# Feed-forward over its inner channels in blocks of 128 in place of 256

## The reference, cut to what matters

```
residual = h
h2 = rmsnorm(h, ln2_w)                                      # (2048, 512)
mlp = jax.nn.silu(h2 @ gate_w) * (h2 @ up_w) @ down_w       # gate, up: (512, 2048); down: (2048, 512)
return residual + mlp
```

## Time and profile before

| | before |
|---|---|
| runs, median (lowest to highest) | 1661.74 us (1661.30 to 1663.65) |
| the profiled execution's own time | 1666.47 us |
| its span, first to last instruction | 1664.8 us |
| mean granted TensorE clock | 0.942 |
| PE busy | 1445.6 us, 87% |
| DVE, ACT, POOL busy | 780.0, 446.8, 441.1 us |
| feed-forward, first matmul to last statistics | 658.4 to 1198.7 us |

### The profile page before, as it was taken

One profiled execution on the slowest core, in us unless ns is written; L12 is line 12 of the kernel. 1 busy time (PEld: TensorE's weight loads), 2 busy tenths in 40 slices (PEclk: granted clock), 3 DMA queues, 4 the chain that ended last, 5 costly groups with the idle time before them and its releaser, 6 DMA issues. The chain is left out here.

```text
span 1664.8 us, 20088 instructions
## 1 busy us (share of the span) xinstructions
PE 1445.6 (87%) x6651; PEld 1045.3 (63%) x6652; DVE 780.0 (47%) x1357; ACT 446.8 (27%) x924; POOL 441.1 (26%) x486
## 2 busy tenths in 40 slices
PE   5688979769999994999999999999760599999996
PEld 4566768536666663888888888888620355555553
DVE  4857676658998992323232323233544122122121
ACT  4333434345555552212112121121120111111110
POOL 2411111126776764101011111010006222222222
PEclk9899999979999997999999999999985799999998
DMA  8112202352332314801000010000197222223220
GB/s 179 51 51 102 101 28 100 127 171 89 107 116 96 121 58 170 289 17 32 20 25 25 16 34 17 22 0 0 53 364 262 87 78 86 87 82 86 89 77 21
DMA packets 92867, 147.12 MB, mean 88 GB/s; under 512 B 29182, under 2 KB 45566, under 8 KB 92800
## 3 DMA queue, kind: packets, MB, share of 16 engines
q1 hardware_dynamic: 79424, 119.92, 22.0%
q0 software_dynamic: 8800, 25.21, 4.5%
q10 hardware_dynamic: 4576, 1.13, 0.3%
HBM read 91.63 MB, written 58.27 MB: 90 GB/s over the span
## 5 line engine op out<-in xcount | busy, mean ns | idle before, releaser
L1356 PE MATMUL ff_bank<-ff_hT_hi,ff_w_hi 128*128 128x512 f32 x512 | 202.3, 395 | 13.3 <-POOL ff_w_lo L1262 13.3
L1356 PE MATMUL ff_bank<-ff_hT_hi,ff_w_lo 128*128 128x512 f32 x512 | 204.9, 400 | 0.0
L1356 PE MATMUL ff_bank<-ff_hT_lo,ff_w_hi 128*128 128x512 f32 x512 | 203.0, 396 | 0.0
L1797 PE MATMUL ex_bank<-w_gu,xT 128*128 x624 | 193.5, 464 | 1.4 <-ACT xT L1728 0.8
L1322 DVE TENSOR_TENSOR ff_prod<-ff_prod,ff_bank 128x512 f32<-128x512 f32 x64 | 44.0, 688 | 274.7 <-PE ff_bank L1356 266.3
L1262 POOL TENSOR_TENSOR ff_w_lo<-ff_stage,ff_w_hi 128x1024 fp32r<-128x1024 f32 x24 | 57.3, 2393 | 417.2 <-ACT ff_w_hi L1309 413.6
L1797 PEld LDWEIGHTS ex_bank<-w_gu,xT 128*128 128x128 f32 x624 | 116.7, 192 | 60.9 <-issue 3.8
L1767 DVE SCALAR_TENSOR_TENSOR result_rows<-ex_bank,xs,result_rows 128x512 f32<-128x512 f32 x39 | 29.3, 751 | 256.2 <-DMA result_rows<-out_dram,xs 253.6
L479 DVE SCALAR_TENSOR_TENSOR conv_acc<-raw,conv_w,conv_acc 128x512 f32<-128x512 f32 x144 | 114.9, 799 | 62.4 <-ACT raw L296 52.5
L572 PE MATMUL pj_bank<-hT_hi,w_in_hi 128*128 128x512 f32 x336 | 140.3, 418 | 1.6 <-DVE hT_lo L412 1.6
L572 PE MATMUL pj_bank<-hT_lo,w_in_hi 128*128 128x512 f32 x336 | 137.5, 409 | 0.0
(11 more groups left out here) (238 smaller groups left out, 2429.9 us busy)
## 6 DMA issues: line engine op xcount, KB each, us to landing
cv_rows<-cst SPq DMA_DIRECT2D x12, 1024.0 KB, 4.3
cv<-cv_rows SPq DMA_DIRECT2D x16, 768.0 KB, 4.3
sorted_rows<-blank SPq DMA_DIRECT2D x1, 10023.0 KB, 46.0
xs<-sorted_rows SPq DMA_DIRECT2D x39, 257.0 KB, 2.7
zs_rows<-zst SPq DMA_DIRECT2D x8, 1024.0 KB, 6.5
zs<-zs_rows SPq DMA_DIRECT2D x16, 512.0 KB, 5.3
w_gu<-in_L_ffn_Wg_dram SPq DMA_DIRECT2D x8, 704.0 KB, 10.7
w_gu<-in_L_ffn_Wu_dram SPq DMA_DIRECT2D x8, 704.0 KB, 11.5
```

The source lines that it names most:

```text
L1356: mm = eng.matmul(ps, w[a], x[b], start=first and i == 0, stop=last and i == 2)
L1797: mm = eng.matmul(ps[:, 0:EI], xT[v % 2][:, k, :], w_gu[:, i, bass.ds(e * KD + k, 1), :].rearrange("p a n -> p (a n)"), start=(k == 0), st ...
```

## The change

FB becomes 128. There are 16 blocks and 64 steps, NI is 1, a step has 24 gate/up matmuls and 12 down matmuls, and the buffers `stage`, `w_hi`, `w_lo`, `p_hi` and `p_lo`, whose sizes are written in FB and NI, are half as large. Each load brings 256 KB in place of 512 KB. Since a step now has only one part, the two gate banks, the two up banks and the two `prod` buffers, which the parts took in turn, are taken by the steps in turn. All waits keep their form; the counts in them follow from NB and NI.

```diff
-FF, FB = 2048, 256
+FF, FB = 2048, 128
...
                     eng.wait_ge(s["gate_ps"], n + 1)
                     eng.wait_ge(s["p_lo"], n + 1)
-                    eng.activation(prod[c][:, :], gate_ps[c][:, :], ACT.Silu).then_inc(s["silu"], 1)
+                    v = (k * NI + c) % 2
+                    eng.activation(prod[v][:, :], gate_ps[v][:, :], ACT.Silu).then_inc(s["silu"], 1)
                     eng.wait_ge(s["prod"], n + 3)
                     eng.wait_ge(s["down"], step * TPR + TPR)
-                    eng.activation(p_hi[k % 2][:, c, :], prod[c][:, :], ACT.Copy).then_inc(s["p_hi"], 1)
+                    eng.activation(p_hi[k % 2][:, c, :], prod[v][:, :], ACT.Copy).then_inc(s["p_hi"], 1)
...
-                    eng.tensor_tensor(prod[c][:, :], prod[c][:, :], up_ps[c][:, :], ALU.mult).then_inc(s["prod"], 1)
+                    v = (k * NI + c) % 2
+                    eng.tensor_tensor(prod[v][:, :], prod[v][:, :], up_ps[v][:, :], ALU.mult).then_inc(s["prod"], 1)
...
-                    eng.tensor_tensor(p_lo[k % 2][:, c, :], prod[c][:, :], p_hi[k % 2][:, c, :].bitcast(F32),
+                    eng.tensor_tensor(p_lo[k % 2][:, c, :], prod[v][:, :], p_hi[k % 2][:, c, :].bitcast(F32),
...
-                    for j, ps, free, done in ((0, gate_ps[c], "silu", "gate_ps"), (1, up_ps[c], "prod", "up_ps")):
+                    for j, ps, free, done in ((0, gate_ps[(k * NI + c) % 2], "silu", "gate_ps"),
+                                              (1, up_ps[(k * NI + c) % 2], "prod", "up_ps")):
```

## The result

The changed kernel takes 1696.12 us (median of 4 runs, 1693.58 to 1697.45), the kernel before 1662.70 beside it (4 runs, 1661.3 to 1665.23): a ratio of 1.0197, 95% interval 1.0179 to 1.0216. It is slower by 33.4 us; forecast were 26.6.

A forecast was written before the change was run, and what follows sets the result against it. PE was taken to bound the feed-forward from end to end; waits at the first border (+11.4), other borders (+11.2) and end (+4.0) summed to +26.6 us, giving 1688 us, range 1679 to 1705.

The forecast's parts named there:

- What bounds the stage: Feed-forward: PE bounds it from end to end; the change can only alter PE's waits at start, borders and end.
- rival C: All 2304 matmuls: narrower weight tiles bring them closer; 11.6 ns less, 231.9 to 220.3, would pay for 26.6 us; chance 0.06.
- The first border: Block 0 to 1: block 1's weights land late behind the clear, ACT's wait stalls PE; +11.4 us, bounds 9.9 to 16.6.
- The twelve slow matmuls: After PE's idle before step 2's out: slow-clock matmuls take 5.2 us, ending just as block 1 can start.
- Rival A: First border: block 1's weights are not late, so it is like the others; +12.0 us, 1674; chance 0.07.
- The borders: Fourteen later block borders: cover halves, the conversion chain shrinks less; 0.80 us each, +11.2 us, bounds 8.8 to 20.3.
- The end: Last block: DVE's additions and statistics behind the last product take 12.8 us; net +4.0 us, bounds 3 and 6.
- The sign named for it: End of stage: last statistics should end about 7.5 us behind PE's last matmul, where today it is 3.5.
- Rival B: Every border: each 0.8 us wait brings back the slow clock, 2.4 us more each; +60 us, 1722; chance 0.05.
- The sum: Whole kernel: first border 11.4, other borders 11.2 and end 4.0 make +26.6 us.

The follow-up runs named there:

- number 7: Changed kernel with 32 unused bytes per partition in front of the feed-forward's weight and product buffers; 1686.92 us (one run).
- number 8: Changed kernel with 32 unused bytes per partition next to the rows of ffT, the weights left in place; 1690.79 us (one run).
- number 9: Kernel before (blocks of 256) with PE waiting for each weight piece by itself and 96 unused bytes before the weights; 1648.51 us against 1664.04, ratio 0.9907.
- number 10: Changed kernel with block 1's loads ahead of the clear, PE waiting for each weight piece, and 96 unused bytes before the weights; 1648.56 us, ratio 0.9910.
- number 11: Changed kernel with 224 unused bytes in front of the weight and product buffers; 1692.92 us (one run).
- number 1: Changed kernel with block 1's three loads issued ahead of the 10 MB clear on SP; 1681.30 us against 1663.39, ratio 1.0114.
- Number 2: Changed kernel with PE waiting for each weight piece before its first reader, not for all three before the block; 1678.52 us, ratio 1.0098.
- Number 4: Changed kernel with DVE computing the last block's third-step statistics twice, its added tile moving the weights by 96 bytes; 1689.60 us (one run).
- number 6: Kernel before (blocks of 256) with PE waiting for each weight piece by itself; 1658.79 us, ratio 0.9973.
- number 5: Changed kernel with block 1's loads ahead of the clear and PE waiting for each weight piece by itself; 1660.38 us against 1663.25, ratio 0.9987.

## Why the prediction came out as it did

*What bounds the stage.* Right: PE, and only its waits changed. The distance of gate/up matmuls was 233.8 ns before (48 of them from 705.44 to 716.66, rows below) and after, so rival C, a closer pace with the change, did not happen. Its idea that operands matter to the distance was right, but the block's size does not set it; the place in memory does (numbers 7 to 11).

*The first border.* Predicted +11.4, measured from the first load's issue: 699.77 - 644.28 = 55.5 us to block 1, where the kernel before had done as many matmuls after 691.45 - 646.79 = 44.7 (691.45 is the prediction's sum; in the trace the next matmul starts at 691.57); +10.8. The links came as told: ACT stood for 22.62 us (over 20 was predicted), the piece took 37.8 us (37.4), PE idled 11.48 (13), and from the landing to block 1 it took 9.27 (9.3). PE did start earlier (8.12 us behind the first load in place of 11.65), and the wait swallowed it. The twelve slow matmuls ran inside the wait, as expected: PE was idle 0.17 us behind them. Rival A did not happen; number 1 shows what it would have been, 18.4 us more stage than before and not 12.0.

*The borders.* The step that was mis-sized: predicted 14 x 0.80 = 11.2, measured 14 x 1.19 = 16.6 us. From the first down matmul the product came at +0.27 (0.20 predicted), its high part at +1.07 (0.92), the weight's at +1.61 (1.46), POOL at +2.30 (2.16) and took 1.33 (1.25), PE followed at +3.76 (3.46). The 0.30 us lie in four links: 0.07 ahead of the product, 0.08 from it to its high part, 0.08 in POOL, whose 1.25 had been the fastest row of another stage (in the changed kernel it took 1.26 in block 0, where DVE had no work yet, and 1.33 here), and 0.08 from POOL to PE (0.13 where 0.05 was taken). Of the excess of 1.19 us over half a block 1.00 is this wait (3.76 - 2.76), 0.10 the first matmul behind it (734.34 to 734.67, 0.33 where 0.233 is the rule), and 0.09 slower down matmuls: twelve take 2.76 us, 230 ns each, where 228 had been read from the kernel before. Number 2 removes the wait and leaves the last of these. The mean rose because a step now has fewer down matmuls, and not because one of them changed. From the kernel before, the first gate/up matmul of a step, then the ninth down matmul behind the first one at 716.66:

```profile
705.44 0.40 PE L1356 MATMUL ff_bank<-ff_hT_hi,ff_w_hi 128*128 128x512 f32 x1
...
718.51 0.39 PE L1356 MATMUL ff_bank<-ff_w_hi,ff_p_lo 128*128 128x512 f32 x1
```

The first eight of an `out` take 1.85 us, 231 ns each, in both kernels (716.66 to 718.51 and 817.59 to 819.44). The others take 227 ns: there are sixteen of them before (718.51 to 722.14) and four after (819.44 to 820.35). The change makes twice as many `out`s and so pays for the slow eight twice as often. In number 10, also of blocks of 128, there are no slow ones, all twelve take 226.7 ns.

*The end.* Predicted +4.0; measured 12.48 us from the last product to the end (12.8 predicted), and +3.8 is left of the stage's difference (31.2 - 10.8 - 16.6); worked out as the prediction did, 5.5 + 12.48 - 14.32 = 3.7. The sign named for it was off: from PE's last matmul to the end it took 6.6 us, not 7.5. Number 4 shows that DVE sets the end.

*The clock.* Rival B did not happen. At the 14 border waits of 0.85 us (the last of 0.69) the granted clock stayed 1.00 (702 to 1215 us). Apart from the start and the end of the stage it was low only around the long idle (0.51 from 694.6 to 699). The Trainium skill (TensorE: Matmul & The Clock Gate, A second HAM failure mode: psum-queue depth-cycling) tells of short idles between groups of matmuls that make the clock swing. Here, with one idle of 0.85 us in 34.58 us, it did not.

*The sum.* 10.8 + 16.6 + 3.8 = 31.2 against 26.6, the end being what the other two leave. The miss is nearly all in the borders. Medians differ by 33.4; the 2.2 us beyond the stage are of the size by which single executions of one kernel differ (3.9 us between the four runs), and no run tells more of them.

## What to carry to other kernels

When a block shrinks, list every wait at its border with the time that covers it: work that halves on the covering engine and only partly on the chain turns into a wait at each border, and its cure was to wait for each piece where it is first read, not to keep the block large. The late transfer's arrival was set by what stood ahead of it in its queue (half as large, it took 37.8 us in place of 40.2); halving the work that hid it made it visible. And before two sizes of a tile are compared, look at the distance of equal matmuls, since buffers that move in memory changed it here by 3%, 12 to 13 us of this stage.

## What the runs showed of the hardware

The distance of matmuls of 128x512 depended on where their operands lie. By the places in each partition modulo 512 bytes of `ffT`'s rows and of the weights (worked out from the order and the sizes of the buffers), and the distance of the gate/up matmuls:

| kernel | rows, weights | ns |
|---|---|---|
| before, after | 480, 384 | 233.8 |
| number 11 | 480, 96 | 232.9 |
| number 7 | 480, 416 | 229.6 |
| number 8 | 448, 384 | 229.6 |
| numbers 4, 9, 10 | 480, 480 | 226.7 |

Equal places are the fastest here, 32 bytes nearer than before already helps, and the order is not one of distance alone (number 11 is 128 bytes apart, before 96). From 233.8 to 226.7 on 1536 gate/up matmuls is 10.9 us; 768 down matmuls add 1.2 in blocks of 256 (from 228.3 ns) and 2.5 in blocks of 128 (from 230). The sums, 12.1 and 13.4, are what the stage lost between numbers 6 and 9 (546.36 to 534.5, 11.9 us) and between numbers 5 and 10 (550.25 to 536.96, 13.3). Equality was tried in one place only, and the buffers behind the weights moved with them. Nor do a matmul's own two operands decide alone: those of the down matmuls lie at equal places in every kernel of the table, and still the first few of each `out` (three in number 11, eight in the changed kernel, ten in numbers 7 and 8) are slow where the gate/up matmuls ahead of them are; in numbers 4, 9 and 10 none is. The mechanism stays open.
